# Hard attention on Trainium2: values multiplied head by head on four column tiles, running sums of eight groups kept in SBUF

## What is computed

```python
Q, K, V = x @ WQ.T, x @ WK.T, x @ WV.T          # each split in 8 heads of 32
attn = Q K^T * 32**-0.5 + (Q we + be)           # per head
attn = softmax(attn + where(adj > 0, 0, -inf))
hard = (attn == max(attn, axis=-1)) / 8         # one key (or equals) a query and head
out  = layernorm(x + hard V)                    # heads side by side, 256 values a row
```

## Time and profile before

| | |
|---|---|
| median of 3 runs | 1510.71 us |
| the profiled execution, whole | 1505.37 us |
| its span, first to last instruction | 1503.6 us |
| granted TensorE clock, mean | 0.929 of 2.4 GHz |
| busy: PE, DVE, ACT, POOL | 79%, 70%, 55%, 49% of the span |
| HBM traffic | 290.88 MB, 193 GB/s |

### The profile page before, as it was taken

How to read it: one execution, slowest core, us unless ns; L and a number is a source line. 1 busy time by engine, 2 the same in 40 slices (tenths; PEclk the granted TensorE clock), 3 DMA queues, 4 the chain that set the end, 5 groups by cost and what they waited for, 6 DMA issues and landing times.

```text
span 1503.6 us, 45448 instructions
## 1 busy us (share of the span) xinstructions
PE 1185.0 (79%) x11346; PEld 899.7 (60%) x11347; DVE 1055.1 (70%) x3140; ACT 830.9 (55%) x1515; POOL 739.0 (49%) x820
## 2 busy tenths in 40 slices
PE   5779588888888888888878787887887888788881
PEld 3334366676666666666667566665665666666661
DVE  4445377777777777777777677777777777777772
ACT  1422365675656655665566465656565656664551
POOL 0000555666666655566555554554454545455550
PEclk9989799999999999899899999989999989999996
DMA  4732577665756666756675666656666676665561
GB/s 143 241 127 97 184 258 216 183 213 185 241 158 224 194 205 199 215 180 204 209 223 160 193 220 192 218 197 199 230 220 214 199 247 199 198 205 157 171 179 42
DMA packets 87215, 290.88 MB, mean 193 GB/s; under 512 B 14688, under 2 KB 27744, under 8 KB 87200
## 3 DMA queue, kind: packets, MB, share of 16 engines
q0 software_dynamic: 48720, 199.60, 42.7%
q1 hardware_dynamic: 38480, 91.11, 17.7%
HBM read 275.97 MB, written 14.68 MB: 193 GB/s over the span
## 4 chain that ended last, share of the span: by engine, by line
DVE 34%; issue 23%; PE 16%; DVEq 12%; DMA 11%; ACT 2%; POOL 1%; POOLq 0%; ACTq 0%; SPq 0%
DMA kv<-kv_table,picks 9%; DVE best L769 8%; DVE reached L741 4%; DVE picks L759 4%; PE ps_s L929 3%; DVE hit L747 3%; PE ps_o L1022 3%; DVE o_run L783 3%; PE ps_s L1010 2%; DVE minus_top L772 2%; PE ps_s L991 2%; DVEq L281 2%; PE ps_s L919 2%; DMA be_sb<-in_L_gnn_be 1%; DVEq L279 1%
## 5 line engine op out<-in xcount | busy, mean ns | idle before, releaser
L398 POOL DMA_INDIRECT kv<-kv_table,picks x609 | 584.6, 960 | 468.9 <-PE ps_o L1022 300.7
L991 PE MATMUL ps_s<-k_t,q_blk 128*128 128x384 f32 x804 | 364.2, 536 | 0.0
L490 ACT ACTIVATE hard<-ps_s,minus_top 128x384 bf16<-128x384 f32 x402 | 211.3, 577 | 234.6 <-DVE minus_top L772 230.2
L389 POOL TENSOR_TENSOR q_blk<-q_t,minus_same 128x256 f32<-128x256 f32 x202 | 152.9, 757 | 262.9 <-issue 157.3
L485 ACT COPY k_t<-ps_s 128x384 f32<-128x384 f32 x404 | 176.2, 483 | 184.5 <-PE ps_s L1010 183.0
L1010 PE MATMUL ps_s<-ident_f,kv 128*128 128x128 f32 x1212 | 184.7, 293 | 88.0 <-DMA kv<-kv_table,picks 81.7
L1022 PE MATMUL ps_o<-kv,hard_t 124*128 124x128 bf16 x3600 | 248.4, 226 | 0.1
L769 DVE TENSOR_REDUCE best<-ps_s 128x1 f32<-128x384 f32 x402 | 204.6, 550 | 36.4 <-PE ps_s L993 19.7
L1022 PEld LDWEIGHTS ps_o<-kv,hard_t 124*128 124x128 bf16 x3600 | 224.5, 102 | 6.2 <-issue 2.7
L475 ACT ACTIVATE hard_t<-ps_h 128x768 bf16<-128x768 bf16 x200 | 162.0, 810 | 112.6 <-PE ps_h L1002 111.9
L783 DVE SCALAR_TENSOR_TENSOR o_run<-o_run,keep,ps_o 128x128 f32<-128x128 f32 x400 | 120.7, 343 | 130.0 <-issue 96.2
(11 more groups left out here) (135 smaller groups left out, 1319.5 us busy)
## 6 DMA issues: line engine op xcount, KB each, us to landing
adj_in<-in_adj SPq DMA_DIRECT2D x128, 512.0 KB, 8.8
kv_table<-kv_out SPq DMA_DIRECT2D x32, 320.0 KB, 2.5
kv<-kv_table,picks POOLq DMA_INDIRECT x609
x_in<-in_x SPq DMA_DIRECT2D x8, 512.0 KB, 7.3
x_row<-in_x SPq DMA_DIRECT2D x32, 128.0 KB
out<-y_out SPq DMA_DIRECT2D x32, 128.0 KB
w<-in_L_gnn_WQ SPq DMA_DIRECT2D x1, 256.0 KB, 3.1
w<-in_L_gnn_WK SPq DMA_DIRECT2D x1, 256.0 KB, 6.1
```

The costliest lines, as they stand in the source:

```text
L398: pool.indirect_dma_start(kv[m % RING][:, c, :], None, kv_table, bass.IndirectOffsetOnAxis(ap=picks[m % RING][:, c, 2:3], axis=0)).then_in ...
L490: done = act.activation(hard[m % 2][:, h, :], ps_s[m % 2][h][:, 0:SLOTS], ACT.Sign, bias=minus_top[m % 2][:, h:h + 1], scale=-1.0)
L991: pe.matmul(bank[:, 0:SLOTS], q_blk[m % 2][:, h, :], k_t[m % 2][:, h, :], start=True, stop=False)
```

## The change

- A value row is stored by head: 8 heads, each its 32 high, 32 middle and 32 low values (`v_part`, `by_head`). ACT and DVE write and read it in pieces of 32.
- `values` multiplies for each half, chunk and head j: the 32 columns of marks of the head with its 96 columns of values (32 of each part), into the 32 PSUM partitions of the head, a column tile of the array. That is 24 matmuls of 32 stationary and 96 moving columns for 18 of 128 and 128. The three parts are no longer summed there.
- The running sum is `o_all`, 8 groups x 2 halves x 96 columns; the group's number modulo 8 chooses the slice, by a register. `merge` works on 96 columns a half, and its wait for `pe_pv` stands on the instruction.
- DVE's and PE's `own_heads` and ACT's `own_rows` go, with their branch; `count_groups` adds the bit to the counter instead.
- At `b` = 0, if rows are due, DVE transposes the four groups of the tile in blocks of 32 x 32 (`turn_rows`, 768 columns, in one of two places by the tile's parity). PE's `rows_back` then has six float32 matmuls with `ident_8` (1/8 on the diagonal) that transpose back and sum the three parts, in place of two transposes. For the last tile `turn_rows` stands after the loop.

```diff
-            return kv_out[k % GT][:, D:ROW].bitcast(BF16)[:, i * D:(i + 1) * D]
+            return kv_out[k % GT][:, D:ROW].bitcast(BF16).rearrange("p (h i c) -> p h i c", h=H, i=PARTS)[:, :, i, :]
...
+        def count_groups(eng, r):
+            eng.reg_add(r["groups"], r["groups"], bits_of(eng, r["began"], 1))
...
-            def merge(m, due):
-                dve.wait_ge(pe_pv, due(pe_pv))
+            def merge(m, due, group):
+                width = PARTS * HD
                 dve.wait_ge(dve_keep, due(dve_keep))
                 for h in range(HALVES):
-                    done = dve.scalar_tensor_tensor(out=o_run[:, h, :], in0=o_run[:, h, :],
-                                                    scalar=keep[m % 2][:, h:h + 1],
-                                                    in1=ps_o[:, h * P:(h + 1) * P], op0=ALU.mult, op1=ALU.add)
+                    o_run = o_all[:].rearrange("p g w -> p (g w)")[:, bass.ds(group * (HALVES * width) + h * width, width)]
+                    done = dve.scalar_tensor_tensor(out=o_run, in0=o_run, scalar=keep[m % 2][:, h:h + 1],
+                                                    in1=ps_o[:, h * width:(h + 1) * width], op0=ALU.mult, op1=ALU.add)
+                    if h == 0:
+                        done._wait_ge(pe_pv, due(pe_pv))
                 done.then_inc(dve_merge, 1)
 
-            def own_heads(m, due):
-                dve.wait_ge(dve_merge, due(dve_merge))
-                dve.tensor_tensor(o_own[:], o_run[:], same[:].unsqueeze(1).to_broadcast([P, HALVES, P]), ALU.mult
-                                  ).then_inc(dve_own, 1)
+            def turn_rows(at, merged):
+                dve.wait_ge(dve_merge, merged)
+                dve.transpose(o_t[:].rearrange("p k (g q) -> p g k q", g=GPT),
+                              o_all[:, at:at + GPT, :].rearrange("p g (k c) -> p g k c", c=HD)
+                              ).then_inc(dve_turned, 1)
...
-                    with group_ended(dve, r):
-                        own_heads(b - 1, for_loop(dve, r, -1))
-                        dve.reg_add(r["groups"], r["groups"], 1)
+                    if b == 0:
+                        with rows_due(dve, r):
+                            odd = bits_of(dve, r["te_done"], 1)
+                            with dve.If_lt(odd, 1):
+                                turn_rows(0, for_loop(dve, r, -1)(dve_merge))
+                            with dve.If_ne(odd, 0):
+                                turn_rows(GPT, for_loop(dve, r, -1)(dve_merge))
+                    count_groups(dve, r)
...
-                    merge(b, for_loop(dve, r, 0))
+                    merge(b, for_loop(dve, r, 0), dve.snap(r["groups"]) & (2 * GPT - 1))
...
-                        for i in range(PARTS):
-                            v = i * D + h * P
-                            mm = pe.matmul(ps_o[:, h * P:(h + 1) * P], hard_t[m % 2][0:USED, at:at + P],
-                                           kv[m % RING][0:USED, c, D:ROW].bitcast(BF16)[:, v:v + P],
-                                           start=(c == 0 and i == 0), stop=(c == CHUNKS - 1 and i == PARTS - 1))
+                        for j in range(HEADS4):
+                            row, v = j * HD, (h * HEADS4 + j) * PARTS * HD
+                            mm = pe.matmul(ps_o[row:row + GQ, h * PARTS * HD:(h + 1) * PARTS * HD],
+                                           hard_t[m % 2][0:USED, at + row:at + row + GQ],
+                                           kv[m % RING][0:USED, c, D:ROW].bitcast(BF16)[:, v:v + PARTS * HD],
+                                           start=(c == 0), stop=(c == CHUNKS - 1))
...
-            def own_heads():
...
             def rows_back(te):
-                pe.wait_ge(act_own, te + 2)
+                pe.wait_ge(dve_turned, te + 1)
                 for h in range(HALVES):
-                    mm = pe.transpose(ps_y[:, h * P:(h + 1) * P], o_t[:, h, :], ident_f[:])
+                    for i in range(PARTS):
+                        mm = pe.matmul(ps_y[:, h * P:(h + 1) * P], o_t[:, h * PARTS + i, :], ident_8[:],
+                                       start=(i == 0), stop=(i == PARTS - 1))
                 mm.then_inc(pe_y, 1)
```

More of the change, by code:

```diff
@@ L93, in hard_attention @@
         earlier_blk = sb("earlier_blk", [P, P], BF16)
-        pick_q = sb("pick_q", [P, GQ], F32)
+        ident_8 = sb("ident_8", [P, P], F32)
         first_f = sb("first_f", [P, NB], F32)
@@ L159, in hard_attention @@
         hard_t = [sb(f"hard_t{i}", [P, HALVES * SLOTS], BF16) for i in range(2)]
-        o_run = sb("o_run", [P, HALVES, P], F32)
-        o_own = sb("o_own", [P, HALVES, P], F32)
-        o_t = sb("o_t", [P, HALVES, P], F32)
+        o_all = sb("o_all", [P, 2 * GPT, HALVES * PARTS * HD], F32)
+        o_t = sb("o_t", [P, HALVES * PARTS, GPT * GQ], F32)
         x_row = sb("x_row", [P, D], F32)
@@ L183, in v_part, with by_head @@
         def v_part(k, i):
-            return kv_out[k % GT][:, D:ROW].bitcast(BF16)[:, i * D:(i + 1) * D]
+            return kv_out[k % GT][:, D:ROW].bitcast(BF16).rearrange("p (h i c) -> p h i c", h=H, i=PARTS)[:, :, i, :]
+        def by_head(values):
+            return values.rearrange("p (h c) -> p h c", h=H)
         ld_w, ld_c, ld_x, ld_row = [sem(f"ld_w{i}") for i in range(3)], sem("ld_c"), [sem("ld_x0"), sem("ld_x1")], sem("ld_row")
@@ L221, in hard_attention @@
         pe_pv, dve_merge = item_sem("pe_pv", 0), item_sem("dve_merge", -1)
-        dve_own, pe_own, act_own, pe_y, dve_y, act_std, dve_row = (
-            sem("dve_own"), sem("pe_own"), sem("act_own"), sem("pe_y"), sem("dve_y"), sem("act_std"),
-            sem("dve_row"))
+        dve_turned, pe_y, dve_y, act_std, dve_row = (
+            sem("dve_turned"), sem("pe_y"), sem("dve_y"), sem("act_std"), sem("dve_row"))
         dve_norm = sem("dve_norm")
@@ L439, in value_high @@
                 act.wait_ge(st_kv[k % GT], 16 * (k // GT)) if k >= GT else None
-                act.copy(v_part(k, 0), ps_s[1][k % 2][:, D:2 * D]).then_inc(v_high, 1)
+                act.copy(v_part(k, 0), by_head(ps_s[1][k % 2][:, D:2 * D])).then_inc(v_high, 1)
             def value_mid(k):
                 act.wait_ge(v_rested, k + 1)
-                act.copy(v_part(k, 1), v_rest[k % 2][:]).then_inc(v_mid, 1)
+                act.copy(v_part(k, 1), by_head(v_rest[k % 2][:])).then_inc(v_mid, 1)
             def cast(f16, f4, i):
@@ L492, in hards @@
                 done.then_inc(act_hard, 1)
[L494 to L497, removed]
             def row_std(te):
@@ L535, in turn @@
                     hards(b + 1, for_loop(act, r, 1))
[L536 to L539, removed]
+                    count_groups(act, r)
                     if b == 0:
@@ L563, in _ @@
             dve.memset(one[:], 1.0)
-            dve.memset(o_run[:], 0.0)
+            dve.memset(o_all[:], 0.0)
             dve.memset(minus_top[1][:], 0.0)
@@ L606, in _ @@
             dve.tensor_tensor(mask_of[:], mask_f[:], mask_g[:], ALU.add)
-            dve.tensor_scalar(pick_q[:], pick_q[:], 1.0 / H, None, ALU.mult)
+            dve.tensor_scalar(ident_8[:], ident_f[:], 1.0 / H, None, ALU.mult)
             dve.tensor_copy(bit[:], power[:].bitcast(F32))
@@ L1019, in values, with rows_back @@
                         at = (h * CHUNKS + c) * P
-                        for i in range(PARTS):
-                            v = i * D + h * P
-                            mm = pe.matmul(ps_o[:, h * P:(h + 1) * P], hard_t[m % 2][0:USED, at:at + P],
-                                           kv[m % RING][0:USED, c, D:ROW].bitcast(BF16)[:, v:v + P],
-                                           start=(c == 0 and i == 0), stop=(c == CHUNKS - 1 and i == PARTS - 1))
+                        for j in range(HEADS4):
[4 more added lines that the diff above has]
+                                           start=(c == 0), stop=(c == CHUNKS - 1))
                 mm.then_inc(pe_pv, 1)
-            def own_heads():
-                at = ((pe.snap(r["groups"]) + 3) & 3) * GQ
+            def rows_back(te):
+                pe.wait_ge(dve_turned, te + 1)
                 for h in range(HALVES):
[L1030 to L1035, removed]
-                pe.wait_ge(act_own, te + 2)
-                for h in range(HALVES):
-                    mm = pe.transpose(ps_y[:, h * P:(h + 1) * P], o_t[:, h, :], ident_f[:])
+                    for i in range(PARTS):
+                        mm = pe.matmul(ps_y[:, h * P:(h + 1) * P], o_t[:, h * PARTS + i, :], ident_8[:],
+                                       start=(i == 0), stop=(i == PARTS - 1))
                 mm.then_inc(pe_y, 1)
@@ L1131, in turn @@
                     values(b, for_loop(pe, r, 0))
-                    with group_ended(pe, r):
-                        pe.reg_add(r["groups"], r["groups"], 1)
-                        own_heads()
+                    count_groups(pe, r)
                     if b == 0:
```

17 lines of the change are left out of this document (5 added, 12 removed).

## The result

The changed kernel took 1553.0 us median (1545.8 to 1557.5, 4 runs) against 1509.8 us for the kernel before beside it: a ratio of 1.0279, 95% interval 1.0229 to 1.0329, +43 us. Timed again on another chip it had 1.0255 (1.0216 to 1.0293), 1539.0 against 1497.6 us. Slower, as forecast, but by nearly three times the forecast's +15.

A forecast was written before the change was run, and what follows sets the result against it. The prediction took DVE with its sequencer as the bound, three quarters of the loop's chain. Terms 39 - 48 + 28 - 6 - 2 + 4 = +15 us gave 1520.4 against 1505.4, forecast as a 1526 us median, range 1487 to 1560.

The forecast's parts named there:

- merge by register: DVE's merge: finding the running sum's slice from a register adds 0.26 us an item over 200 items, +39 us.
- factor 0.75: DVE and its sequencer hold three quarters of the loop's chain, so each DVE step counts 0.75 of its length.
- price of 0.26: Register work per item in us: 0.20 before the merge's first half, +0.06 for the second half and narrower width.
- TensorE's and the transfers' quarter: The quarter of the loop's chain not DVE's: 166 us of PE, 127 of DMA, some 45 of ACT and POOL.
- Own heads, `rows_back` and transposes: DVE's own heads gone -48 us, block transposes +28, PE's own heads gone with `rows_back` added -2.
- 0.28 us was expected in all plain items: Sign of a right forecast: DVE's `bits` to `best` near 0.28 us in every plain item.
- Values: PE's values products: 1.0 us for 1.17, counted on some 38 values on the chain, -6 us.
- bound of -27: Lower bound of the values term, in us; rival 2 uses it with values at 0.5 us.
- issue-paced 1.0: PE's 24 values matmuls at 0.043 us each at most take 1.0 us, against about 0.5 side by side.
- rival 2: Column tiles side by side shorten values to 0.5 us, gathers start earlier, stalls shrink: -14 us, 1497 us; chance 0.13.
- rival 3: PE's tile mode empties the array and the clock falls, values take 1.6 us: 1572 us; chance 0.10.
- After the loop: Transposes (1.0 us) and `rows_back` (some 2.9 us) come serially behind DVE's loop, +4 us.

The follow-up runs named there:

- constant slice: The changed kernel with every merge at one constant-addressed slice (output incomplete): 1524.9 us, 1.0060; on a third chip 1478.3 us, 0.9851.
- Slot kept: The changed kernel with the slice's number taken before `best` instead of between `keep` and the merge: 1537.5 us, 1.0258.
- Register slice alone: The kernel before, its 128-column merge through a register-addressed slice (output incomplete): 1561.5 us, 1.0288; on a fourth chip 1563.4 us, 1.0432.
- tiles only: The kernel before with values by head on column tiles and 96-column merges, own heads kept (output incomplete): 1527.6 us, 1.0075; third chip 1479.8 us, 0.9857.
- Save on ScalarE: The changed kernel merging between two constant sums, ScalarE copying each item's sum to its group's slice: 1540.6 us, 1.0151; fourth chip 1490.1 us, 0.9952.

## Why the forecast had the direction and not the size

**The merge by register is the step that failed most: predicted +39, measured +61.** Its price an item was right; the factor 0.75 on it was wrong. The chain of waits of one item, from `keep` on, in the changed kernel on the third chip (start us, us, what):

```profile
708.87 0.07 DVE keep L764
...
709.97 0.14 DVEq L725
710.11 0.05 issue
710.16 0.04 DVEq L773
710.20 0.03 issue
710.23 0.06 DVEq L773
710.29 0.06 issue
710.35 0.09 DVE o_all L773
710.44 0.08 issue
710.52 0.15 DVEq L879
710.66 0.08 DVE o_all L773
710.74 0.03 issue
710.78 0.28 DVEq L297
711.06 0.06 issue
711.12 0.33 DVE hit L736
```

The same item's turn in the constant-slice version, same chip:

```profile
682.41 0.07 DVE keep L764
...
683.49 0.11 DVEq L725
683.60 0.05 issue
683.65 0.02 DVEq L770
683.67 0.05 issue
683.73 0.21 DVE o_all L773
683.94 0.02 issue
683.96 0.06 DVE o_all L773
684.02 0.03 issue
684.05 0.28 DVEq L297
684.33 0.06 issue
684.39 0.33 DVE hit L736
```

Read both from `keep` to `hit`. `keep` to the merge's first half is 1.48 us against 1.32: +0.16, near my 0.20. From there to `hit` it is 0.77 against 0.66: +0.11, where I had put 0.06 because the second half's address "lies beside the first half". It does, but the counter's step (L879) and the branch after it (L297) then wait behind it: in the constant version the branch starts 0.32 us after the merge, here 0.43. Over the 197 items that can be paired in the timeline, `keep` to merge grew from 320.5 to 347.2 us and merge to `hit` from 152.4 to 178.3: 53 of the 61 us. So 0.27 us an item, as the price of 0.26 said, the first half a little cheaper and the second dearer. What was wrong is the factor 0.75: the item's register steps were counted at VectorE's share of the chain. Slot kept shows why that share is the wrong factor. Moving one step took `keep` to merge down to 325.0 us, and `bits` to `best` went from 224.3 to 236.0 and `hit` to `bits` from 305.8 to 309.0; the whole was -1.5 us by the medians. Wherever in the item the step stands, the sequencer pays it. The slack that I expected of TensorE's and the transfers' quarter shows only in the 29 items that have front-end steps between `keep` and the merge: there that stretch did not grow (-4.5 us in all, while VectorE's wait of L678 for TensorE fell from 21.4 to 5.3), in the 171 others it grew by 31.8. Register slice alone on the kernel before (+64) has the same price.

The rest of the 61 us is not one thing. Between the two traces (1476.9 and 1538.4 us) 4.2 us lie ahead of the first `keep` (at 170.7 and 174.9 us; the three traces with a constant slice have 170.1 to 170.7, all others 172.6 to 175.9, and no run tells why) and 3.1 after the last merge (below). In the loop `hit` to `bits` adds 10.1 (295.7 to 305.8 us), and `bits` to `best` gives back 4.6. Of `hit` to `bits` it is L730 that grew, here in the groups by line of the constant slice:

```profile
L730 DVE TENSOR_SCALAR reached<-iota_h,ends_of 128x384 bf16<-128x384 f16 x205 | 79.0, 385 | 1.7 <-issue 1.7
```

and of the changed kernel on the same chip:

```profile
L730 DVE TENSOR_SCALAR reached<-iota_h,ends_of 128x384 bf16<-128x384 f16 x205 | 87.7, 428 | 1.7 <-issue 1.7
```

Its plain duration is 0.31 us, but 29 of 205 took over 0.5 in the one and 46 in the other, and the long ones lie beside GpSimd's work (last section). That the shifted timing makes them more frequent is seen in single items there; no run tests it.

**Own heads, `rows_back` and transposes: predicted -22, measured -1.5.** 31 more transposes cost 1.0038 - 0.9851 = 0.0187 (about 0.004 either way, across two chips), 28 us, the number forecast. In part that is luck: the forecast had 1.2 us each with branches and a wait, times 0.75; what was doubled is the bare transpose, and its 0.9 us is paid in full. `rows_back` and the tail are inside the rest. So own heads with TensorE's part of them were worth some 29 us, not 50. On VectorE's timeline the step looks better than that: `bits` to `best` went from 238.9 us (tiles only) to 228.9 (constant slice) with the 28 us of transposes in it, which makes 38 us for the multiply and its branch, against 48 predicted. But the 48 had the factor 0.75 in it, and without it the sizes were too good throughout: 0.45 us a group's end was expected, and the ends without transposes gave 0.34 where nothing else stood between `bits` and `best` (50 items) and 0.21 where layernorm or lists did (52). 0.28 us was expected in all plain items, and in the changed kernel's trace on that chip 37 of 93 have it; nearly all the others took 0.44 or more. That those still jump a branch over rows or lists is argued from the code. I had taken a saving from one pair of items and applied it to all. Of the other 9 us the tail is 1.4. The rest may lie in the executions traced: the one of tiles only was its slowest (1492.0 us, 12 above its median), so the timelines make this step 13 us where the medians make it 1.5. It stays open.

**Values: predicted -6, measured -18** (-16 to -27 by the ratio's interval), at the bound of -27 or short of it. The four tiles do run side by side: 0.44 us, the lower bound and not the issue-paced 1.0. "0.043 us a small matmul at most" was read from matmuls with full weights; 24 with 32-column weights take 0.018 each. The gain came the way rival 2 said: waits of the kernel before, on the third chip,

```profile
PE ps_s L1010 <- DMA kv<-kv_table,picks: 80.0, 34, 13.7
...
DVE pay L689 <- PE ps_o L1022: 37.3, 12, 5.6
```

and of the tiles alone:

```profile
PE ps_s L1013 <- DMA kv<-kv_table,picks: 65.5, 29, 13.7
...
DVE pay L692 <- PE ps_o L1025: 16.9, 7, 4.3
```

Values that end earlier free the gathers' buffers earlier, TensorE waits 15 us less for gathers, and VectorE 20 us less for TensorE at the front end. The second is the surer sign: that wait is 37.3 to 43.8 us in the three traces of the kernel before and 13.7 to 16.9 in the three with shorter values, while TensorE's wait for gathers is back at 84.3 in the constant slice, which is as fast. Rival 2's mechanism was at work inside a forecast that had it at 0.13. Of rival 3 (mode change, falling clock) only the clock came: it was 0.898 to 0.914 in the changed kernel's first runs. But it fell to 0.900 in the tiles' trace too, and that version was faster than the kernel before at 0.921; the constant slice, at 0.908 to 0.919, gains.

The Trainium skill's two pages differ here as the prediction told: "TensorE: Matmul & The Clock Gate", part 3, is the one that the trace bears out (1.17 to 0.44 us, 2.7 times, with the column count per head also changed); of the drain in "TensorEngine Tiling (Array Packing)" these rows show nothing, since the 24 products with their neighbours cost no more than six full-width ones.

**After the loop: predicted +4.** From the last merge's start to `y` it is 28.1 us in the changed kernel and, by the rows of the same places on the third chip, 23.6 before. The size was right, its parts were not, so this is partly luck: the constant slice has 25.0, with the same transpose and `rows_back`. The other 3.1 us lie in the 37 empty passes that the loop still makes; no merge runs in them, and the sequencer's instructions are the same, but a pass takes 0.67 us in the changed kernel and 0.58 to 0.59 with the constant slice (0.70 and 0.58 before, for the outer and the inner loop). Why is open.

**The sum.** 12 us better in the values, 20 worse in the own heads (with transposes and `rows_back`), 22 worse in the merge, and the tail's +4 is inside these: 15 - 12 + 20 + 22 - 4 = 41, against 1539.0 - 1497.6 = +41.4.

## What to carry to other kernels

Where an engine's sequencer fills the gaps between its steps, expect a register step to cost its whole length in every item, wherever it is put, as here; do not discount it by that engine's share of the chain. Try such addressing on an engine whose sequencer has room (ScalarE here), and keep the bound engine on constant slices. Before a loss is laid to a part of a change, profile the unchanged kernel on the same chip beside it.

## What the runs showed of the hardware that I had not expected

**TensorE's signals can be late on one chip and not on another, with the same program.** Tiles alone: 676 of 1648 late by more than 0.15 us (760 us in all, the longest 2.8) and a ratio of 1.0075; the same code on another chip: 0 of 1784 and 0.9857. Constant slice: 668 of 1541 and 1.0060; 1 of 1647 and 0.9851. Save on ScalarE: 1.0151 and 0.9952. The register slice went the other way, 1.0288 and 1.0432. The profile shows it as waits for "remote" or an unknown queue. Whether the kernel before has late signals on that chip was not profiled there, and what sets them off stays open; that they end just behind GpSimd's gathers is all that the traces tell; with 501 late the changed kernel still had nearly the ratio it has without (1.0279 and 1.0255).

**VectorE's `reached` is held up by GpSimd's `q_blk`, if that started first.** One item of the changed kernel, third chip, both engines:

```profile
1308.98 0.73 POOL L389 TENSOR_TENSOR q_blk<-q_t,minus_same 128x256 f32<-128x256 f32 x1 [0.96 <-PE ps_s L989]
1309.10 0.73 DVE L730 TENSOR_SCALAR reached<-iota_h,ends_of 128x384 bf16<-128x384 f16 x1
```

The same item with the constant slice:

```profile
1257.67 0.31 DVE L730 TENSOR_SCALAR reached<-iota_h,ends_of 128x384 bf16<-128x384 f16 x1
1257.83 0.73 POOL L389 TENSOR_TENSOR q_blk<-q_t,minus_same 128x256 f32<-128x256 f32 x1 [0.96 <-PE ps_s L989]
```

0.73 us for a step of 0.31 where `q_blk` began 0.12 us ahead, 0.31 where it began 0.16 behind. In the changed kernel's trace 38 of the 46 long ones end 0.11 to 0.13 us after a `q_blk` ends. Of the 36 that start while `q_blk` runs 29 are long, of the 30 during which it starts 4. The Trainium skill, "SBUF — State Buffer", section "Who interferes with whom", says that VectorE and GpSimd share one pair of ports as an exclusive lock. The rows fit that, but no version here took `q_blk` away to show it.

**A block transpose costs what a plain copy of its width would:** 128 x 768 float32 in 0.977 us, written in pieces of 32 to six places, where the estimate from plain rows was 0.95 (1.04 ns a column, and their fixed part); other strides were not tried; a second one directly behind the first adds 0.87 us (`bits` to `best` 2.24 for 1.39 us).
